# Moving a histogram into one of two gather loops, and turning the layout of ScalarE's per-edge terms

## The reference, cut to what matters

```python
# L1: per edge h, per node four statistics over its incoming edges
h = jnp.concatenate([xi, xj, ea], axis=-1) @ Wpre + bpre
s1 = jax.ops.segment_sum(h, dst, num_segments=n_nodes)
s2 = jax.ops.segment_sum(h * h, dst, num_segments=n_nodes)
mn = jnp.where(has, jax.ops.segment_min(h, dst, num_segments=n_nodes), 0.0)
mx = jnp.where(has, jax.ops.segment_max(h, dst, num_segments=n_nodes), 0.0)
# L3: messages of both directions, divided by how many there are.
m0 = T[rel0, idx0] + biases[l][rel0]
m1 = T[rel1, idx1] + biases[l][rel1]
```

## Time and profile before

| | |
|---|---|
| median of 3 runs | 2839.73 us (2839.11 to 2842.17) |
| the profiled execution | 2844.6 us |
| its span, first to last instruction | 2842.8 us |
| loop 0, first to last start of L2039 | 186.6 to 1288.6 us |
| loop 1, first to last start of L2198 | 1385.1 to 2442.1 us |
| busy share of the span | PE 50%, DVE 73%, ACT 43%, POOL 63% |
| TensorE clock granted, mean of the span | 0.602 of 2.4 GHz |

### The profile page before, as it was taken

How to read it: one execution, slowest core, us unless ns; L and a number is a source line. 1 busy time by engine, 2 the same in 40 slices (tenths; PEclk the granted TensorE clock), 3 DMA queues, 4 the chain that set the end, 5 groups by cost and what they waited for, 6 DMA issues and landing times.

```text
span 2842.8 us, 30745 instructions
## 1 busy us (share of the span) xinstructions
PE 1425.1 (50%) x4575; PEld 609.9 (21%) x4583; DVE 2072.2 (73%) x3688; ACT 1214.8 (43%) x3258; POOL 1779.8 (63%) x1794
## 2 busy tenths in 40 slices
PE   2225555666645454435444444444333422389994
PEld 1101111121111111113211111111111100287552
DVE  6857777887766667677688888888677877844376
ACT  0013344343434344443355566656555555431222
POOL 3457777776677777771577777767777777203012
PEclk7556666566556666565555555555555555569996
DMA  5232222222222222230222222222212211108430
GB/s 137 58 84 65 63 63 68 62 59 63 57 69 65 69 67 70 70 71 22 52 60 57 62 59 59 62 65 58 59 47 60 56 30 31 46 1 303 140 110 7
DMA packets 133278, 192.18 MB, mean 68 GB/s; under 512 B 71759, under 2 KB 87588, under 8 KB 133056
## 3 DMA queue, kind: packets, MB, share of 16 engines
q0 software_dynamic: 57424, 91.61, 14.9%
q1 hardware_dynamic: 47604, 70.70, 7.9%
q10 hardware_dynamic: 28189, 29.18, 3.0%
HBM read 148.38 MB, written 39.84 MB: 66 GB/s over the span
## 4 chain that ended last, share of the span: by engine, by line
issue 23%; DVE 22%; POOL 16%; PE 16%; DVEq 9%; ACT 6%; DMA 5%; POOLq 2%; ACTq 0%; SPq 0%
POOL arena L589 15%; PE mm L775 4%; ACT arena L1418 4%; DVE red L2076 3%; PE l L835 3%; DVE red L2187 3%; DVE arena L2062 2%; DMA arena<-kv_tab,rec 2%; PE hist L1005 2%; DVE score L2042 2%; DVEq L2075 2%; PE mm L927 2%; PE tp L1005 2%; DMA arena<-b_tab,lin 2%; DVE T L2033 1%
## 5 line engine op out<-in xcount | busy, mean ns | idle before, releaser
L589 POOL DMA_INDIRECT arena<-b_tab,lin x815 | 810.7, 995 | 292.0 <-issue 269.0
L589 POOL DMA_INDIRECT arena<-kv_tab,rec x815 | 813.5, 998 | 278.7 <-issue 229.6
L835 PE MATMUL l<-arena,identB 128*128 128x512 bf16 x990 | 407.9, 580 | 489.0 <-DVE arena L2062 441.1
L1418 ACT ACTIVATE arena<-arena,lin 128x64 f32<-128x64 f32 x1984 | 479.6, 333 | 0.0
L2187 DVE TENSOR_REDUCE red<-arena 128x128 f32<-128x2048 f32 x189 | 459.6, 2486 | 13.7 <-issue 12.8
L927 PE MATMUL mm<-Wshared,eaT 48*128 48x512 f32 x248 | 234.2, 1097 | 401.9 <-ACT eaT L1412 390.9
L2062 DVE TENSOR_SCALAR arena<-arena,digit 128x512 bf16<-128x512 int16 x744 | 257.8, 415 | 56.3 <-PE l L835 42.9
L857 PE MATMUL hist<-arena,oh_lo 125*128 125x225 bf16 x400 | 170.6, 583 | 234.5 <-DVE arena L2033 234.5
L835 PEld LDWEIGHTS l<-arena,identB 128*128 128x128 bf16 x996 | 114.0, 128 | 774.8 <-DVE arena L2062 548.7
L1415 ACT ACTIVATE arena<-arena 128x1024 f32<-128x1024 f32 x62 | 65.6, 1057 | 434.0 <-DVE arena L2210 434.0
L1332 ACT ACTIVATE T<-arena,negcode 128x512 f32<-128x512 int16 x248 | 164.6, 711 | 164.3 <-issue 164.3
(11 more groups left out here) (408 smaller groups left out, 2412.7 us busy)
## 6 DMA issues: line engine op xcount, KB each, us to landing
arena<-at_tab SPq DMA_DIRECT2D x50, 800.0 KB, 4.5
at_tab<-T ACTq DMA_DIRECT2D x25, 800.0 KB, 3.5
arena<-kv_tab,rec POOLq DMA_INDIRECT x815
arena<-b_tab,lin POOLq DMA_INDIRECT x815, 2.5
at_pack<-arena SPq DMA_DIRECT2D x25, 256.0 KB
T<-at_pack SPq DMA_DIRECT2D x25, 256.0 KB
lin_tab<-lin ACTq DMA_DIRECT2D x62, 64.0 KB, 1.6
lin<-lin_tab SPq DMA_DIRECT2D x62, 56.0 KB
```

Of the source, the lines that this page charges most:

```text
L589: return pool.indirect_dma_start(dst, None, table, offs(ap=index, axis=0))
L835: last = pe.matmul(l3[:, 0, :], identB[:], hot[:, j], start=False, stop=True, skip_group_check=True)
L1418: last = act.activation(dst[:, s], hh[u][:, s, 0:C], ACT.Identity, bias=bias[:, s:s + 1])
```

## The change

The whole histogram goes into loop 1: its first 50 steps each take two groups, one after the other, and loop 0 has none, so one body serves all its pairs and the tiles of constants ahead of it go. In loop 1 the squares get a tile of their own. It and the tiles for maximum and minimum have their slots innermost: the 16 slots of a feature are neighbours. ACT therefore writes with a step of 16 words from one element to the next, and DVE reduces three of four tiles along adjacent words. h itself keeps its layout, [slot][feature], but without the squares between its rows, and gets a reduction of its own, so that there are four of 1,024 elements in the place of one of 2,048 and two of 1,024.

```diff
-        hh = [at(4160 + 4240 * u, P, SLOTS, 2 * C) for u in range(2)]
-        hmax = [at(6352 + 4240 * u, P, SLOTS, C) for u in range(2)]
-        hmin = [at(7376 + 4240 * u, P, SLOTS, C) for u in range(2)]
+        hh = [at(4160 + 4240 * u, P, SLOTS, C) for u in range(2)]
+        hsq = [at(5184 + 4240 * u, P, C, SLOTS) for u in range(2)]
+        hmax = [at(6352 + 4240 * u, P, C, SLOTS) for u in range(2)]
+        hmin = [at(7376 + 4240 * u, P, C, SLOTS) for u in range(2)]
...
# PE
-            def count_types(n, g, u):
+            def count_types(g, u):
                 pe.wait_ge(hist_oh, g + 2)
                 for j in range(8):
-                    last = pe.matmul(hist[:, 0:NB * R], oh_lo[:, u, :, j], oh_hi[n][u][:, :, j],
+                    last = pe.matmul(hist[:, 0:NB * R], oh_lo[:, u, :, j], oh_hi[u][:, :, j],
                                      start=False, stop=True, skip_group_check=True)
                 last.then_inc(hist_mm, 1)
...
-                    if with_hist:
-                        count_types(0, 2 * i + u, u)
...
                 if with_hist:
-                    count_types(1, 2 * i + u + 2 * HI, u)
+                    for j in range(2):
+                        count_types(2 * (2 * i + u) + j, j)
...
# ACT
                     act.wait_ge(h_ready, 2 * i + u + 2)
-                    act.activation(hh[u][:, :, C:2 * C], hh[u][:, :, 0:C], ACT.Square)
+                    act.activation(hsq[u].rearrange("p c s -> p s c"), hh[u], ACT.Square)
                     for dst, bias in ((hmax[u], neg[u]), (hmin[u], pos[u])):
                         for s in range(SLOTS):
-                            last = act.activation(dst[:, s], hh[u][:, s, 0:C], ACT.Identity, bias=bias[:, s:s + 1])
+                            last = act.activation(dst[:, :, s], hh[u][:, s], ACT.Identity, bias=bias[:, s:s + 1])
...
# DVE
-            dve.tensor_copy(lane_of[0], bc(laneI[0:ROW], 8))
-            dve.tensor_copy(code_of[0], bc(codeI[0:ROW], 8))
...
-                if with_hist:
-                    type_hots(0, 2 * i + u, 8 * (2 * i + u), u)
...
             dve.memset(hh[1], 0.0)
+            dve.memset(hsq[1], 0.0)
...
                 dve.wait_ge(hmin_ready, g + 1)
-                for t, acc, op, r in parts:
-                    red_(r, t.rearrange("p s c -> p c s"), X_AXIS, op)
+                red_(red[:, 0:C], hh[u].rearrange("p s c -> p c s"), X_AXIS, ALU.add)
+                for t, op, k in ((hsq[u], ALU.add, 1), (hmax[u], ALU.max, 2), (hmin[u], ALU.min, 3)):
+                    red_(red[:, k * C:(k + 1) * C], t, X_AXIS, op)
...
                 if with_hist:
-                    type_hots(1, 2 * i + u + 2 * HI, 8 * (2 * i + u) + 16 * HI, u)
+                    for j in range(2):
+                        type_hots(2 * (2 * i + u) + j, j)
```

More of the change, by code:

```diff
@@ L203, in build @@
         hots = lambda v: v[0:ROW].bitcast(BF16).rearrange("p (c j) -> p c j", j=8)
-        oh_hi = [[hots(T1[:, 1024 + 900 * u:1924 + 900 * u]) for u in range(2)],
-                 [hots(arena[:, o:o + 900]) for o in (1120, 25400)]]
-        lane_of = [hots(arena[:, o:o + 512]) for o in (22860, 12768)]
-        code_of = [hots(arena[:, o:o + 900]) for o in (20474, 3140)]
+        oh_hi = [hots(arena[:, o:o + 900]) for o in (1120, 25400)]
+        lane_of = hots(arena[:, 12768:12768 + 512])
+        code_of = hots(arena[:, 3140:3140 + 900])
         part = at(24000, ROW, NROW)
@@ L861, in _, with step0 @@
             pairs = pe.value_load(totI[0:1, 0:1], min_val=HI + 1, max_val=STEPS // 2 - 8)
-            def step0(i, u, with_hist):
+            def step0(i, u):
                 if True:
@@ L876, in step0 @@
                         transpose_counts(finished(word))
-                    if with_hist:
-                        count_types(0, 2 * i + u, u)
-            with aligned(pe, 0, HI) as i:
+            with aligned(pe, 0, pairs) as i:
                 for u in range(2):
-                    step0(i, u, True)
-            with aligned(pe, HI, pairs) as i:
-                for u in range(2):
-                    step0(i, u, False)
+                    step0(i, u)
             pe.wait_ge(ohA_ready, 2 * pairs + 1)
@@ L2027, in _, with type_hots, step0 @@
             d().then_inc(oh_ready, 1)
-            def type_hots(n, g, t, u):
+            def type_hots(g, u):
                 dve.wait_ge(hist_mm, g + 1)
-                cols = bass.ds(t, 8)
-                tt(oh_lo[:, u], lane_of[n], bm(partB[:, cols], P), ALU.is_equal)
-                tt(oh_hi[n][u], code_of[n], bm(codeB[:, cols], NB * R), ALU.is_equal).then_inc(hist_oh, 1)
-            def step0(i, u, with_hist):
+                cols = bass.ds(8 * g, 8)
+                tt(oh_lo[:, u], lane_of, bm(partB[:, cols], P), ALU.is_equal)
+                tt(oh_hi[u], code_of, bm(codeB[:, cols], NB * R), ALU.is_equal).then_inc(hist_oh, 1)
+            def step0(i, u):
                 blk = step_head(LOOP0, i, u)
@@ L2082, in _ @@
             pairs = dve.value_load(totI[0:1, 0:1], min_val=HI + 1, max_val=STEPS // 2 - 8)
-            with aligned(dve, 0, HI) as i:
+            with aligned(dve, 0, pairs) as i:
                 for u in range(2):
-                    step0(i, u, True)
-            with aligned(dve, HI, pairs) as i:
-                for u in range(2):
-                    step0(i, u, False)
+                    step0(i, u)
             for u in range(2):
@@ L2165, in _ @@
             dve.memset(accS, 0.0)
-            dve.tensor_copy(lane_of[1], bc(laneI[0:ROW], 8))
-            dve.tensor_copy(code_of[1], bc(codeI[0:ROW], 8))
+            dve.tensor_copy(lane_of, bc(laneI[0:ROW], 8))
+            dve.tensor_copy(code_of, bc(codeI[0:ROW], 8))
             dve.wait_ge(mm_evac, ring["mm"])
@@ L2182, in add_step @@
                 blk = block_in(before)
-                parts = ((hh[u], accS, ALU.add, red[:, 0:2 * C]), (hmax[u], accMx, ALU.max, red[:, 2 * C:3 * C]),
-                         (hmin[u], accMn, ALU.min, red[:, 3 * C:4 * C]))
+                parts = ((accS, ALU.add, red[:, 0:2 * C]), (accMx, ALU.max, red[:, 2 * C:3 * C]),
+                         (accMn, ALU.min, red[:, 3 * C:4 * C]))
                 dve.wait_ge(hmin_ready, g + 1)
-                for t, acc, op, r in parts:
-                    red_(r, t.rearrange("p s c -> p c s"), X_AXIS, op)
+                red_(red[:, 0:C], hh[u].rearrange("p s c -> p c s"), X_AXIS, ALU.add)
+                for t, op, k in ((hsq[u], ALU.add, 1), (hmax[u], ALU.max, 2), (hmin[u], ALU.min, 3)):
+                    red_(red[:, k * C:(k + 1) * C], t, X_AXIS, op)
                 d()
-                for t, acc, op, r in parts:
+                for acc, op, r in parts:
                     v_ = acc[:, bass.ds(blk, 1), :]
@@ L2195, in step1 @@
                 blk = block_in(word[u])
-                h = hh[u][:, :, 0:C]
+                h = hh[u]
                 wait_rows(LOOP1, u)
```

## The result

The changed kernel took **2816.86 us** (median of 4 runs, 2815.65 to 2822.83), the kernel before 2839.42 beside it. The ratio is 0.9923, 95% interval 0.9911 to 0.9936: faster by 0.8%. Forecast were 2829, in a range of 2808 to 2854, and faster with 0.58. The profiled execution took 2822.83 us, against 2844.6: 21.8 less, where my sum had 11 less.

A forecast was written before the change was run, and what follows sets the result against it. DVE or POOL was taken to bound loop 0's steps, with ACT's chain also bounding alternate middle steps of loop 1. Loop 0 -31 and loop 1 +20 gave -11: 2834 us profiled, 2829 as median, range 2808 to 2854.

The forecast's parts named there:

- Loop 0, -31: Loop 0 without the histogram: middle 24 steps 412.6 to 390 us (-23), 25 POOL-bound steps 0.33 each (-8).
- rival of a loop 0 without gain: Loop 0's middle is held by the records' way through ACT and gains nothing: -8 + 20, total 2852; chance 0.06.
- Reductions, -1.95: Loop 1, DVE: three reductions reading slots innermost take 1.22 us instead of 1.875 each, -1.95 us a step.
- Square, +1.1: Loop 1, ACT: Square, writing with a step of 16 words, takes 1.1 us longer.
- The 32 short activations hidden: Loop 1, ACT: the stepped writes of the 32 short activations, 0.13 us each, are hidden within starts every 0.24 us.
- The rival of 3.4 us a step: Loop 1, ACT: all 33 instructions pay for stepped writes, 3.4 us a step, total 2909; chance 0.08.
- Middle pair 34.1, +9: Middle of loop 1: a short and a long step take 15.1 + 19.0 = 34.1 us against 33.3, x12 = +9.
- Last steps +4, tail -1: End of loop 1: three steps go from 13.8 to 15.1 us (+4); tail: Square +1.1, DVE's last reductions -1.95 (-1).
- POOL, +8: Loop 1: POOL meets L2033 twice a step, +0.33 us in 25 POOL-bound steps, +8.
- PE hidden: Loop 1: with eight more matmuls, 3.40 us, PE's path takes 14.5 us, under DVE's 15.1, so hidden.
- rival of a rising clock: Loop 1: more counting raises PE's clock from 0.50, four matmuls save 1.2 us a step, total 2811; chance 0.07.
- an ACT that pays nothing: Loop 1: ACT pays nothing for stepped writes, pair 15.1 + 17.9 = 33.0, loop 1 +2, total 2811; chance 0.15.

The follow-up runs named there:

- the move alone: Against the kernel before, the whole histogram moved into loop 1, with ACT, the reductions and the tile layout left as before: 2843.94 us, ratio 1.0013.
- the layout alone: Against the kernel before, the tile layout and reductions changed, the histogram left in both loops: 2849.18 us, ratio 1.0023.
- one matmul of eight: Against the changed kernel, one counting matmul of each histogram group's eight kept, DVE's one-hots kept, most counts left out: 2818.98 us, ratio 0.9918.

## Why the prediction was right, and where its sizes were off

The direction and the mechanism held: loop 0 gives more than loop 1 takes, because the reductions make room on DVE. The sum was half of what came: -11, and the profile has -21.8. Within each loop some terms came out near their values for partly other reasons, as said below.

- **Loop 0, -31; measured -36.8.** The POOL-bound steps gave 8.2, and the end 0.3, where I had 8. The middle gave 28.2 where I had 23: I had worked out 380 us from the gathers and DVE's 15.54, then added 10 for window fetches and for records on ACT's queue. Measured are 384.4, so these cost 4. This is the largest miss of the sum, 5 us. The rival of a loop 0 without gain falls.
- **Ahead of loop 0, nothing.** DVE's first instruction of loop 0 starts at 186.59 in the changed kernel, after 15.5 us of waiting for its gathered rows, and at 186.62 before: the casts were hidden.
- **Histogram on DVE, +1.65 a step.** 17.04 - 15.39 = 1.65, shown by the move alone.
- **Reductions, -1.95.** 1.21 us each for three, 1.96 for the one that stays in steps; the short step falls from 17.04 to 14.99, by 2.05, where I had 15.1 left.
- **Square, +1.1.** Measured +0.92, below the bracket of 1.2 to 1.8 that L1542 gave and above DVE's 0.65. The value chosen was between the rows and rightly so, but L1542, which also reads PSUM, was no good measure of a stepped write. On the chain only 0.78 us of it show (17.94 to 18.72), since the next activation starts 1.77 us after Square's start and not 1.97. What the Trainium skill ("Vector Engine (DVE) Microarchitecture Reference", "Measured stream behaviour on trn2") has for a VectorE destination at 24 words gave an estimate of +1.7: ScalarE paid about half of that, 0.9 ns an element, at 16 words written as at 64 read.
- **The 32 short activations hidden.** 7.74 us before and 7.75 after in the timeline, though their mean grew by a fifth. The rival of 3.4 us a step falls. The mean alone would have misled here.
- **Middle pair 34.1, +9.** Measured 33.7 and +5.5. The long step was 18.7 and not 19.0, by the size of Square.
- **Last steps +4, tail -1.** In the last three steps the chain went from 13.98 to 14.73 us, by 0.75 a step and not by 1.3: +2.2. But DVE's first instruction of a step did not follow it: from step 58 to step 61 the starts take 40.9 us in place of 41.4, and the whole end zone is 1.2 shorter. The lateness came out as a wait for the edge product in the last step, 3.26 us where it was 0.46. Behind that the tail did what I had forecast: Square +0.8, the last reductions -1.9. Together the tail is 1.7 longer. DVE's last reductions, which I had taken to have nothing beside them, also wait for ACT:

```profile
2425.91 1.22 DVE L2201 TENSOR_TENSOR arena<-arena,mm 128x1024 f32<-128x1024 f32 x1 [3.26 <-PE mm L922]
...
2436.69 1.87 DVE L2176 TENSOR_REDUCE red<-arena 128x64 f32<-128x1024 f32 x1 [3.61 <-ACT arena L1414]
```

  Before, that last wait was 0.88 us. Sum of both terms: +3 forecast, -1.2 + 1.7 = +0.5 measured.
- **POOL, +8.** Measured 3.1 early and 5.8 late, 8.9. That this is near 8 is partly luck. The move alone has 5.3 and 3.3 there, 8.6, as forecast; but the layout alone, with as many one-hots in loop 1 as before, has 1.5 and 3.6, and the two together stay at 8.9. Also, the slow gather is no matter of L2033 alone, as I had read it: 81 of the 97 in loop 1 are held by L2026, the shorter one-hot.
- **PE hidden.** Shown by one matmul of eight. **The clock** stayed at 0.50 in loop 1, so the rival of a rising clock falls; its total, 2811, lies nearer to the result than mine, by chance.

In sum: 5.8 us of the miss of 10.8 lie in loop 0, 3.5 in the middle of loop 1 and 2.5 at its end and in the tail, less 0.9 of POOL. The gap between the loops (+0.5) and what lies outside them (-0.5) cancel. The lower end of the range, 2808, was put down to an ACT that pays nothing, but the sum of that rival is 2811; the measured 2817 lies inside either way.

## What to carry to other kernels

Two edits that each gain nothing can gain together, when one frees time on an engine that has slack already and the other brings work that can use the slack: price them jointly, step kind by step kind. Where short and long steps alternate and a different engine bounds each, moving a cost between those engines changes nothing; the gain needs a third place for the work. Of the group means, check those of overlapping instructions against the timeline before believing that they grew. And where gathers share the time with DVE, look at which instruction's end a slow gather follows: here it is each time one with both inputs in SBUF.

## What the runs showed of the hardware

- ACT's Square of 128x1024 float32 takes 1,057 ns contiguous, 1,974 ns writing at a step of 16 words and 1,976 ns reading at a step of 64: +0.9 ns an element, the same on either side. The next activation starts 0.96, 1.77 and 1.89 us after its start. In 64-element activations issued back to back the stepped write cost no time in sequence: 32 take 7.74 us contiguous and 7.75 stepped.
- DVE's reduction of 1,024 elements takes 1.21 us reading adjacent words and 1.88 us (maximum and minimum, kernel before) to 1.96 us (sum, changed kernel) in steps of 64 words.
- POOL's issue of a gather takes 0.94 us mostly. One that starts 0.2 us or more into a DVE instruction with both inputs in SBUF, float32 or bfloat16, ends 0.80 to 0.83 us after that instruction (all 212 gathers over 1.06 us in the changed kernel, up to 1.91 us), with or without most of PE's counting matmuls. One input in PSUM (L2201) or a single input (L2176) does not hold it: 0.94 to 0.95 us.
- The granted clock of TensorE stayed at 0.50, its 1.2 GHz level, in the middle of loop 1 with PE busy 259 of 400 us, and was 0.61 in loop 0 with 177 of 412. More work did not raise it.
